# A cross-attention and mixture-of-experts block: another order of its first and last attention steps, and five opening loads issued from ScalarE

## What is computed

```python
x = x + tanh(g_xattn) * attention(layernorm(x), ctx, ctx)   # 16 heads of 64, rope, window 64
x = x + tanh(g_ffn) * experts(layernorm(x))                 # 2 shared, 16 routed, top 4
# attention: softmax(mask(rope(q) @ rope(k).T / 8)) @ v, then @ wo.T
# experts:   sum_s gelu(x @ up_s.T) @ down_s.T + sum_r gate_r * (gelu(x @ up_r.T) @ down_r.T)
# gate:      softmax(x @ router.T), all but the 4 largest set to 0
```

## Time and profile before

| | us |
|---|---|
| median of 3 runs | 535.01 (534.13 to 536.21) |
| the profiled execution | 534.29 |
| its span | 532.5 |
| PE busy | 513.2 |
| DVE, ACT, POOL busy | 339.8, 311.8, 280.0 |
| clock granted to TensorE | 1.0 (2.4 GHz) |

### The profile page before, as it was taken

One profiled execution on the slowest core, in us unless ns is written; L12 is line 12 of the kernel. 1 busy time (PEld: TensorE's weight loads), 2 busy tenths in 40 slices (PEclk: granted clock), 3 DMA queues, 4 the chain that ended last, 5 costly groups with the idle time before them and its releaser, 6 DMA issues.

```text
span 532.5 us, 13139 instructions
## 1 busy us (share of the span) xinstructions
PE 513.2 (96%) x4904; PEld 453.9 (85%) x4904; DVE 339.8 (64%) x1062; ACT 311.8 (59%) x861; POOL 280.0 (53%) x225
## 2 busy tenths in 40 slices
PE   9868989999999999999999899999999999999997
PEld 6656888899889988888889789989999999999996
DVE  5768876657675676667675837665646465645444
ACT  3465876565766567765866766664455445544442
POOL 2899898779887968987998415430200020000000
PEclk9999999999999999999999999999999999999999
DMA  8441233111031101120221074306400540036001
GB/s 270 118 133 41 76 78 121 33 36 37 2 115 36 38 2 36 57 57 12 65 57 41 19 238 139 100 1 198 162 1 1 192 166 1 2 127 233 0 1 39
DMA packets 21613, 41.02 MB, mean 77 GB/s; under 512 B 3056, under 2 KB 5360, under 8 KB 21552
## 3 DMA queue, kind: packets, MB, share of 16 engines
q1 hardware_dynamic: 21552, 40.20, 24.3%
HBM read 30.62 MB, written 2.23 MB: 62 GB/s over the span
## 4 chain that ended last, share of the span: by engine, by line
PE 76%; DVE 9%; ACT 5%; POOL 4%; issue 4%; DMA 1%; SPq 0%; DVEq 0%; ACTq 0%; POOLq 0%
PE ring L895 52%; PE psS L895 9%; PE psO L1098 5%; PE psS L1067 4%; PE psT L1079 4%; ACT prob L590 2%; DVE wl L777 1%; DVE arena L706 1%; DVE arena L709 1%; PE psT L1044 1%; ACT pT L599 1%; POOL arena L428 1%; DVE arena L832 1%; DMA craw<-in_ctx 1%; POOL prob L444 1%
## 5 line engine op out<-in xcount | busy, mean ns | idle before, releaser
L895 PE MATMUL ring<-xTh,wh 128*128 128x512 f32 x272 | 112.1, 412 | 1.7 <-DVE xTl L668 1.7
L895 PE MATMUL ring<-xTh,wl 128*128 128x512 f32 x272 | 107.1, 394 | 0.0
L895 PE MATMUL ring<-xTl,wh 128*128 128x512 f32 x272 | 107.0, 393 | 0.0
L895 PE MATMUL ring<-wh,oTh 128*128 128x256 f32 x272 | 78.4, 288 | 2.1 <-DVE oTl L846 1.4
L895 PE MATMUL ring<-wl,oTh 128*128 128x256 f32 x272 | 76.8, 282 | 0.0
L895 PE MATMUL ring<-wh,oTl 128*128 128x256 f32 x272 | 76.7, 282 | 0.0
L444 POOL TENSOR_TENSOR prob<-prob,rinv 128x512 f32<-128x512 f32 x64 | 68.6, 1072 | 13.9 <-DVE rinv L842 13.8
L536 ACT ACTIVATE oTh<-prob 128x512 fp32r<-128x512 f32 x64 | 40.4, 631 | 53.7 <-PE ring L895 24.8
L764 DVE TENSOR_TENSOR oTl<-prob,oTh 128x512 fp32r<-128x512 f32 x64 | 44.7, 698 | 41.9 <-ACT oTh L536 41.7
L520 ACT ACTIVATE sneg<-ring 128x512 f32<-128x512 f32 x72 | 43.0, 597 | 38.4 <-PE ring L895 38.0
L756 DVE TENSOR_TENSOR prob<-sneg,arena 128x512 f32<-128x512 f32 x64 | 47.4, 741 | 27.6 <-ACT sneg L520 27.6
(11 more groups left out here) (118 smaller groups left out, 1259.4 us busy)
## 6 DMA issues: line engine op xcount, KB each, us to landing
arena<-gate_scratch SPq DMA_DIRECT2D x64, 256.0 KB, 5.7
raw<-in_e SPq DMA_DIRECT2D x18, 256.0 KB, 2.6
raw<-in_w SPq DMA_DIRECT2D x16, 256.0 KB, 3.2
arena<-arena SPq DMA_DIRECT2D x16, 256.0 KB, 3.1
arena<-arena SPq DMA_DIRECT2D x16, 192.0 KB, 3.4
out<-x SPq DMA_DIRECT2D x16, 128.0 KB, 5.7
x<-in_x SPq DMA_DIRECT2D x3, 512.0 KB, 4.5
craw<-in_ctx SPq DMA_DIRECT2D x3, 512.0 KB, 3.5
```

The costliest lines, as they stand in the source:

```text
L895: last = pe.matmul(out, a, b, start=start and i == 0 and j == 0, stop=stop and i == n - 1 and j == 2, skip_group_check=check)
```

## The change

Same arithmetic, other order, in four parts.

1. **Loads.** The two halves of x, the identity, cos and sin of the first batch are issued by ACT as its first five instructions, and no longer by SP between the weight pieces.
2. **Opening.** k is now rotated by halves on DVE in every unit. In the hand-written opening DVE puts rotations ahead of weight rests, and the maxima of chunks 4 and 5 ahead of q of unit 2; POOL takes weight piece 5 after the four rotations of unit 0; PE does `transpose_probs(0)` before `scores(2)` and q of unit 2 before `values(0)`; ACT copies transposition 1 before the exponential of chunk 2. The addition of eps and the negation of the mean move from POOL to DVE.
3. **Loop.** On ACT, at odd steps, the second copy of a transposition comes before the step's jobs, and no longer after them.
4. **Drain.** The loop ends at chunk 60; chunks 61 to 63, the router of batch 0 and the first four experts are written out by hand.

```diff
+CLOSING = 61
...
-        for c in range(OPENED, CHUNKS + 4):
+        for c in range(OPENED, CLOSING):
...
+            for half in range(2):
+                part = slice(2 * half, 2 * half + 2)
+                act.dma_start(x[:, 0, part, :], x_d[0][:, part, :]).then_inc(in_x0[half], 16)
+            act.dma_start(ident[:, :], ident_d).then_inc(in_ident, 16)
+            act.dma_start(cos[:, :], cos_d).then_inc(in_rope, 16)
+            act.dma_start(sin[:, :], sin_d).then_inc(in_rope, 16)
             for job in (("w", 0), ("ctx", 0), ("w", 1), ("w", 2), ("w", 3), ("xT", 0), ("w", 4), ("w", 5),
                         ("v", 0), ("w", 6)):
                 do(job)
...
-                if c < CHUNKS:
-                    softmax_numerator(c)
-                if not ahead:
-                    for job in jobs:
-                        do(job)
+                softmax_numerator(c)
                 if c in transposed:
                     copy_transposed(transposed[c] + 1)
+                for job in jobs:
+                    do(job)
...
-                last.then_inc(ln_stat, 1)
+                link(last)
+                if j:
+                    dve.tensor_scalar(nmean[:, :], mv[:, :, 0], -1.0, None, ALU.mult)
+                dve.tensor_scalar(vare[:, :], mv[:, :, 1], EPS, None, ALU.add).then_inc(ln_stat, 1)
...
+            if kind == "k" or u == 0:
+                return [(rotated(kind, u, pair), slice(pair, pair + 1)) for pair in range(2)]
+            return [(rotated(kind, u), slice(0, 2))]
...
+            transpose_probs(58)
+            do(("r", 0))
+            transpose_probs(59)
+            scores(62)
+            values(29)
+            transpose_probs(60)
+            expert(0)
+            do(("y", UNITS - 2))
+            do(("gT", 0))
+            transpose_probs(61)
+            expert(1)
+            values(30)
+            transpose_probs(62)
+            expert(2)
+            transpose_probs(63)
+            down(0)
+            values(31)
+            expert(3)
+            do(("y", UNITS - 1))
+            down(1)
```

More of the change, by code:

```diff
@@ L360, in _ @@
                 sp.dma_start(craw[:, kc, :], ctx_d[0][:, kc, :]).then_inc(in_ctx0[kc], 16)
-            for half in range(2):
-                part = slice(2 * half, 2 * half + 2)
-                sp.dma_start(x[:, 0, part, :], x_d[0][:, part, :]).then_inc(in_x0[half], 16)
             load_piece(1)
-            sp.dma_start(ident[:, :], ident_d).then_inc(in_ident, 16)
             load_piece(2)
-            sp.dma_start(cos[:, :], cos_d).then_inc(in_rope, 16)
-            sp.dma_start(sin[:, :], sin_d).then_inc(in_rope, 16)
             load_piece(3)
@@ L399, in _ @@
                     do(job)
-                for job in drained(c):
-                    do(job)
-            for n in range(4, N + 2):
+            for quarter in range(4):
+                do(("spread", quarter))
+            for n in range(2, N + 2):
                 for job in after[n]:
@@ L872, in _ @@
                                       rw_parts[:, :, 0, :].bitcast(F32), ALU.subtract).then_inc(rw_lo, 1)
-                if c < CHUNKS and c % 2 == 0:
+                if c % 2 == 0:
                     score_max(c)
                     score_max(c + 1)
-                if c <= CHUNKS:
-                    invert(c - 1)
+                invert(c - 1)
                 if c in attended:
                     rest_att(attended[c])
-                for job in jobs + drained(c):
+                for job in jobs:
                     do(job)
+            invert(60)
+            router(0)
+            score_max(62)
+            score_max(63)
+            invert(61)
+            rest_att(29)
+            pick_a(0)
+            pick_b(0)
+            invert(62)
+            invert(63)
+            do(("y", UNITS - 2))
+            do(("gT", 0))
+            rest_att(30)
+            expert(1)
+            rest_gated(1)
+            rest_att(31)
+            gated(2)
+            for job in after[2]:
+                do(job)
+            expert(3)
+            do(("y", UNITS - 1))
+            for job in after[3]:
+                do(job)
             for n in range(4, N + 2):
```

141 lines of the change are left out of this document (71 added, 70 removed).

## The result

The changed kernel took 537.02 us (median of 22 executions), the kernel before 535.73 us beside it (22 executions). The ratio is 1.0029, with a 95% interval of 1.0020 to 1.0039: 1.6 us more by the ratio (1.3 by the medians), well inside the half per cent that the prediction took for "the same". The forecast was 531.2, so it missed by 5.8 us and had the wrong sign. Two of the changed kernel's executions, at 625 and 1743 us, and one of the kernel before, at 630, are left out of the ratio. A second set of the same kernel (`e0_after_again`, 12 executions) gave 536.67 against 535.67 (1.0021, 1.0008 to 1.0035), near the 537.0 and 1.003 expected of it; 7 of its 12 executions had a granted clock of 0.994 or less, so the first set had not met an unlucky lot of low clocks.

The account below looks back on a forecast made before the run. TensorE, busy 513.2 of 532.5 us, was taken as the bound, with POOL close behind in the opening. Opening with loads -3.1, loop 0 and drain -0.7 gave -3.8 from 535.01: 531.2 us, range 528.5 to 535.0.

Parts of the forecast that it names:

- The clock is at its full level in all of them: TensorE's stretches 14 to 79, 79 to 290 and 290 to 306 us: full clock, so no term for it.
- Term 1: Loads up to the first q: a later context and two small DVE operations move q from 16.43 to 18.0, +1.6 us.
- the bounds 0 and 1.9: Shift of the context's landing: 0 if SP's transfers keep their times, 1.9 us if queues share equally; 1.4 taken.
- the wait of 1.0 that I expected before `scores(0)`: Opening: PE ends k of unit 1 at 23.5 while POOL rotates q's first half until 24.4, a new wait of 1.0.
- The opening, -3.1 at 79 us: Start to 79 us, the later first q included: shorter waits put PE 3.1 us ahead.
- The allowance of 0.6 us: POOL up to division 5: about 0.6 us for one more meeting with DVE and a short wait for the first `invert`.
- paced by POOL: Rival, chance 0.24: PE gives its opening wins back at POOL's divisions; opening wins 1.5, drain nothing, time 533.5 us.
- Term: 0: Loop, 79 to 290 us: k by halves and the later context rounding are hidden, 0 us.
- The drain, -0.7: Drain: idle 1.8 us against 2.4 and 0.1 won before, -0.7 us, bounds -1.5 and +0.6.
- ACT held by its commands: Rival, chance 0.09, slower: five commands over 0.9 us each delay the opening; at 2.5 us each, 539.2 us.
- Undisturbed loads: Rival, chance 0.15: the loads don't disturb each other, the context keeps its 6.05, time 529.0 us.

Follow-up runs that it names:

- e6: The kernel before without its single matmul on zeros between the transposition of x and the first q: 536.16 us, ratio 1.0017 to the kernel before.
- e1: The changed kernel with DVE again rotating the second half of k of unit 0 ahead of the rests of x: 534.36 us, 0.9974 of the kernel before.
- e7: The changed kernel with ACT's jobs (context, weight piece 14) ahead of the second copy at chunk 11 alone: 534.39 us, 0.9982 of the kernel before.
- e4: The changed kernel with ACT's jobs ahead of the second copy again in the whole loop: 534.19 us, 0.9974 of the kernel before.
- e3: The changed kernel with x, identity, cos and sin issued by SP again: 535.70 us, 0.9996 of the kernel before.
- e9: The kernel before with only x, identity, cos and sin of the first batch moved to ACT's queue: 536.75 us, ratio 1.0024 to the kernel before.

## Why the prediction was wrong

**"The clock is at its full level in all of them"**, and so no term for it: this step failed, and it is the largest, 1.49 + 1.17 = 2.7 of the 6.45 us between -3.8 and +2.65. The profile of before showed one execution without a fall of the clock, and I took that for a property of the kernel. The order lengthened the idle time in front of q (1.73 to 2.86 us), and PE ran at 1.2 GHz behind it, as in 7 of the 8 profiles with so long a wait there and in none of the 5 with a shorter one. The zero matmul that stands at this very place, and its removal in e6, point the same way. For the 1.17 in the drain the cause stays open; the runs show its price and that it comes with the changed drain.

**Term 1, the front, +1.6: near in sum, wrong in its parts.** q came at +2.03; that this is near is luck, since two errors of opposite sign make it. The context moved by 0.73 to 0.83 instead of 1.4, a little under the middle of the bounds 0 and 1.9: an equal share of the engines for two queues, which gave the upper bound, overstates it more than twofold. What I left out is the other part: I wrote that DVE ends the rest of x and then the second half of k, and let q start after the former. q takes the ring tile that this second half is read from, so it starts after the latter, 1.2 us later. The code says it: a job may write its ring tile once the job two places earlier has been read out. e1 shows it by itself. At v of unit 1 this came out even (28.71 at full clock against 28.55), since the wait of 1.0 that I expected before `scores(0)` did not come: a second error that cancels the first by luck.

**The opening, -3.1 at 79 us: measured -1.25 at full clock.** The mechanism was right: the wait before v of unit 1 went from 2.90 to 0.40, that of 67.71 vanished, and POOL then sets the pace. The allowance of 0.6 us for meetings and waits of POOL was too small. At full clock POOL starts the second rotation at 18.01 and ends division 5 at 55.76; by the forecast's sum of work (53.66 - 19.00 + 1.30 - 0.72 = 35.24) that would be 53.25. So 2.5 us went to what I had put at 0.6: 1.3 us of idle, 1.12 of it before the first division, which waits for the late scores, and 1.2 of longer instructions (for instance 2.92 for 2.42 and 1.80 for 1.31). That puts the transposition that takes this division at 55.82 instead of 54.5; behind it the removed waits gave 0.95 instead of 1.5. The rival "paced by POOL" described this half: it put the opening's gain at 1.5.

**The loop, "Term: 0": wrong by 1.8.** I followed the context's rounding behind the copy, and found its rest on POOL covered, which it is. I did not follow the other job of the same step, weight piece 14, whose rest on DVE now begins just behind POOL's and takes 1.6 us longer than before (2.86 for 1.24); the maxima stand behind it. A step that is moved takes all its jobs along, and each needs its own look: e7 restores this one step and gets 2.6 us back, 1.7 of it as idle time of PE in the loop. That k by halves costs the loop nothing was right: e4 and e7 keep it.

**The drain, -0.7: right, the clock apart.** At full clock, in e7, it measures 27.06 - 27.59 = -0.53. Two waits came as forecast, 0.25 and 1.07 for 0.2 and 1.05; the third, 0.55 before `values(29)`, was 0.27 in e7; none came before y of unit 14. The gates were issued at 314.5 and not 311.5, since PE was late by then (2.01 us at the scores of chunk 60, 1.17 more by the clock), and cost nothing: from 306 to 400 us the one wait of PE in the profile is 0.2 us for DVE.

**The rivals.** ACT held by its commands is refuted: 0.45 to 0.58 us each. Undisturbed loads are refuted by e3 and e9, one in each direction.

Sum of the misses: clock 2.66, opening 1.85, loop 1.77, drain 0.17, together 6.45. Against the median of before, which holds a fall of the clock in most executions, the kernel loses a little less than that.

## What to carry to other kernels

When a wait before a matmul gets longer, ask for the clock behind it too, and take the clock from many executions: one profile at full level does not say that the kernel keeps it. When a job moves in an order, list all that it carries (here a weight rounding beside the context), and for each what starts beside it on the engine that can hold it up, as VectorE and GpSimd do here. And a tile that is taken in turn is a dependence like any other: the reader that is put behind other work holds the next writer.

## What the runs showed of the hardware

The granted clock differs between executions of one kernel on one chip, and sorts their times: the changed kernel took 537.06 us at 0.993 (11 of its 20) and 535.54 at 0.996 (3), the kernel before 535.87 at 0.997 and 534.20 at 1.0. One stretch at half level cost 1.5 us in the opening and 1.17 in the drain.

Such a stretch began in or just behind an idle time of 2.59 to 2.86 us in 7 of 8 profiles, and after 1.73 us or less at the same place in none of 5. In the drain it came after waits of no more than 1.07 us.

A rest that takes 0.69 us on VectorE while GpSimd does nothing took 2.86 when GpSimd had begun a two-input operation 0.08 us before it, and 1.24 when a shorter one had begun 0.35 before; both times it ended 0.54 us after GpSimd's. In the other order GpSimd's 2.40 became 2.85. Here the one that begins second pays.

Five transfers on a second queue, issued at the same time, delayed the rounding of the first queue's context by 0.7 to 0.9 us: 6.05 became 6.78 in the changed kernel and 6.88 in e9, and going back made it 5.92.
